# A macaron block (MoE FFN, attention, MoE FFN): a region per expert in the dispatch buffer, routing by batch, routed tiles in pairs, both FFNs' edges interleaved with attention

## The reference

```python
x = x + 0.5 * ffn(layernorm(x))        # routed and shared experts
x = x + attention(layernorm(x))        # 16 heads of 128, weights codes * scales
x = x + 0.5 * ffn(layernorm(x))

def ffn(flat):                          # 2048 tokens, 16 experts, top 2
    probs = softmax(flat @ router_w.T)
    topk_w, topk_idx = top_k(probs, 2);  topk_w = topk_w / sum(topk_w)
    shared = silu(flat @ shared_gate_w) * (flat @ shared_up_w) @ shared_down_w
    routed[t] = sum_k topk_w[t, k] * expert[topk_idx[t, k]](flat[t])
    return shared + routed              # an expert: silu(x @ gate) * (x @ up) @ down, inner width 128
```

## Time and profile before

| | us |
|---|---|
| median of 3 runs | 1320.77 (1317.02 to 1323.13) |
| span of the profiled execution | 1325.7 |
| PE busy in it | 1119.1 |
| DVE busy | 906.1 |
| ACT busy | 758.1 |
| POOL busy | 328.3 |

### The profile page before, as it was taken

How to read it: one execution, slowest core, us unless ns; L and a number is a source line. 1 busy time by engine, 2 the same in 40 slices (tenths; PEclk the granted TensorE clock), 3 DMA queues, 4 the chain that set the end, 5 groups by cost and what they waited for, 6 DMA issues and landing times. The chain is left out here.

```text
span 1325.7 us, 22540 instructions
## 1 busy us (share of the span) xinstructions
PE 1119.1 (84%) x5904; PEld 932.2 (70%) x5905; DVE 906.1 (68%) x1903; ACT 758.1 (57%) x1645; POOL 328.3 (25%) x421
## 2 busy tenths in 40 slices
PE   2556894589999999999999999999999994666884
PEld 1356783478888878888878887887888873455783
DVE  5654565677777777777777777777777778753554
ACT  3433551466767666666666676766676664433551
POOL 2174551750000351000144000042000001373551
PEclk9777997699999999999999999999999997877997
DMA  7563344430000131000032000028000001253435
GB/s 228 161 189 111 117 125 131 131 104 25 17 25 25 47 91 47 24 17 24 29 83 72 24 16 24 16 71 224 24 18 7 1 0 57 83 184 102 122 116 191
DMA packets 108557, 102.80 MB, mean 78 GB/s; under 512 B 13364, under 2 KB 97339, under 8 KB 108480
## 3 DMA queue, kind: packets, MB, share of 16 engines
q1 hardware_dynamic: 62880, 63.02, 17.1%
q10 hardware_dynamic: 37920, 22.07, 5.8%
q0 software_dynamic: 7680, 16.87, 3.4%
HBM read 54.55 MB, written 35.82 MB: 68 GB/s over the span
## 5 line engine op out<-in xcount | busy, mean ns | idle before, releaser
L198 PE MATMUL bank<-R 128*128 (+2 forms) x1056 | 416.6, 395 | 74.5 <-DVE R L539 47.2
L199 PE MATMUL bank<-R 128*128 (+2 forms) x1056 | 384.8, 364 | 0.0
L200 PE MATMUL bank<-R 128*128 (+2 forms) x1056 | 383.8, 363 | 0.0
L198 PEld LDWEIGHTS bank<-R 128*128 128x128 f32 x1056 | 207.8, 197 | 120.8 <-DVE R L539 43.7
L1048 DVE TENSOR_REDUCE a_mx<-bank 128x1 f32<-128x512 f32 x256 | 172.4, 691 | 99.5 <-PE bank L200 96.9
L200 PEld LDWEIGHTS bank<-R 128*128 128x128 f32 x1056 | 208.0, 197 | 29.7
L199 PEld LDWEIGHTS bank<-R 128*128 128x128 f32 x1056 | 208.9, 198 | 22.5
L974 ACT ACTIVATE work<-bank,a_mx 128x512 f32<-128x512 f32 x256 | 175.1, 688 | 55.3 <-DVE a_mx L1048 54.8
L980 ACT ACTIVATE R<-bank 128x512 fp32r<-128x512 f32 x256 | 139.1, 596 | 89.1 <-PE bank L1169 81.2
L1041 DVE SCALAR_TENSOR_TENSOR R<-bank,a_bslot,R 128x512 fp32r<-128x512 f32 x192 | 143.5, 747 | 64.6 <-ACT R L968 62.6
L1063 DVE TENSOR_TENSOR R<-bank,R 128x512 fp32r<-128x512 f32 x256 | 167.9, 680 | 11.0 <-ACT R L980 8.4
(11 more groups left out here) (137 smaller groups left out, 1528.1 us busy)
## 6 DMA issues: line engine op xcount, KB each, us to landing
R<-R ACTq DMA_DIRECT2D x60, 256.0 KB, 2.7
work<-in_ffn_w SPq DMA_DIRECT2D x54, 256.0 KB, 3.3
work<-xs_dram SPq DMA_DIRECT2D x96, 129.0 KB, 2.1
work<-y_dram SPq DMA_DIRECT2D x16, 512.0 KB, 5.0
work<-in_codes SPq DMA_DIRECT2D x64, 128.0 KB, 2.0
work<-in_scales SPq DMA_DIRECT2D x256, 32.0 KB, 1.8
xs_dram<-empty ACTq DMA_DIRECT2D x6, 1032.0 KB, 14.9
xs_dram<-empty SPq DMA_DIRECT2D x6, 1032.0 KB, 14.8
```

Of the source, the lines that this page charges most:

```text
L198: nc.tensor.matmul(out, ah, bh, start=(i == 0), stop=False)
L199: nc.tensor.matmul(out, ah, bl, start=False, stop=False)
L200: last = nc.tensor.matmul(out, al, bh, start=False, stop=(i == n - 1))
```

## The change

The kernel is written anew as one block with one instruction list per engine, and no hardware loops; every tile and unit is written out.

- **A region per expert.** `xs_dram` has 16 regions of 2048 + 128 rows, one for each expert, and 128 spare rows. A token's row is its region's base plus its rank in the expert, so that a batch's rows are known when the batches up to it are ranked. Rows are scattered per batch and choice (8 groups of 4). SP fills 128 rows behind each expert's last row with empty ones (16 DMAs at addresses read from `frow`), and loads tiles from addresses read from `toff`.
- **Routing by batch.** Statistics, normalizing, transposes, logits (now directly as [tokens, experts]), choice, ranks and positions run for one batch of four tiles after another. rstd comes by Ln and Exp on ACT and one Newton step.
- **Tiles in pairs.** 24 pairs instead of 48 tiles; one ACT or DVE operation for two tiles; a word is loaded for four tiles. ACT alone copies results out, without the weight; `combine` multiplies by the weight, 8 DVE operations a batch in place of 2. 16 tile buffers instead of 8.
- **Edges.** `EARLY` is 2. After the first FFN's tiles only batch 0 is combined, normalized and transposed before attention, and batch 1 while it starts; batches 2 and 3 follow at the end of units 0 and 2, and their transposes behind units 2 to 5. The attention's result is added to X directly (output projection as [tokens, values]: 12 matmuls of 256 columns for 6 of 512; no transposes back). The second FFN's statistics, transposes, logits, choices and positions of batches 0 to 2 run in units 52 to 63, its normalizing and scatters on POOL. All four shared steps come before the second FFN's tiles.
- **Weights of the second FFN.** The shared ones stay. The routed ones are split a second time by POOL during attention (16 experts, 768 columns), written to `w_dram`, and loaded as attention frees their place.

The core of the diff:

```diff
-NSLOT_TILES = (NTOK * TOPK + NE * (P - 1)) // P
-NR = -(-NSLOT_TILES // 4) * 4
+REGION = NTOK + P
+SPARE = NE * REGION
+XROWS = SPARE + P
+ROW = D + 1
+NR = 48
+NPAIR = NR // 2
...
+    x_load(0)
+    sp.dma_start(m.cst[:], t["consts"]).then_inc(s["cst_in"], 16)
+    x_load(1)
...
+    for c in range(2, NCHUNK):
+        chunk(c)
...
+    def fills(f):
+
+        sp.wait_ge(s[f"frow{f}"], 1)
+        for e0 in range(0, NE, 8):
+            _, at = nc.values_load_multi_w_load_instructions(
+                m.frow[0:1, e0:e0 + 8], engines=[SP_ENGINE], min_val=0, max_val=XROWS - P)
+            for v in at:
+                sp.dma_start(m.xs_dram[f][bass.ds(v, P), :], t["empty"]).then_inc(s[f"fill{f}"], 16)
...
+    fills(0)
+    tile_loads(0)
+    for n in range(4):
+        part(n)
+    results_landed(0)
+    y_loads(0, 0, 0)
...
+    weights(0)
+    for e in range(FIRST_PRE):
+        presplit(e)
+    weights(1)
...
+    for u in range(UNITS):
+        more = u + 1 < UNITS
...
+        act.wait_ge(s["o"], u + 1)
+        wait(act, s["y"], u)
...
+        if u in (0, 2):
+            b = 2 + u // 2
+            rstd("a", b)
+            normalize("a", b, xna(b), range(QB))
+        if u in (52, 56, 60):
+            rstd("1", (u - 52) // 4)
...
+        if u >= 4 and u % 4 == 0:
+            y_add(u // 4 - 1)
+        bias_lo(1, m.oT, "o", u, 2)
+        if u in (0, 2):
+            b = 2 + u // 2
+            combine(0, b, 0, 32 * (b + 1))
+            statistics("a", b)
+            rstd("a", b)
+        if u in (52, 56, 60):
+            q = (u - 52) // 4
+            dve.wait_ge(s["y_add"], 13 + q)
+            st.settle()
+            statistics("1", q)
+            rstd("1", q)
+        if u in L1_BEHIND and more:
+            choose(1, L1_BEHIND[u], te3(bank[0][:, 0:64]))
+        if u in R1_BEHIND:
+            positions(1, R1_BEHIND[u], te3(bank[0][:, 0:64]))
...
+    for step in range(2, QB):
+        gate_up(1, 2 * step)
+        gate_up(1, 2 * step + 1)
+        down(1, step)
+    pe.wait_ge(s["x_add"], 4 * QB)
+    pe.wait_ge(s["e_in"], 16 * NE)
+    tiles(1)
```

```diff
+    def behind_done(u):
+        if u in V_BEHIND:
+            pe.wait_ge(s["v_lo"], V_BEHIND[u] + 1)
...
+        if u in L1_BEHIND and u + 1 < UNITS:
+            pe.wait_ge(s["l_read1"], L1_BEHIND[u] + 1)
+        if u in R1_BEHIND:
+            pe.wait_ge(s["pos1"], TOPK * R1_BEHIND[u] + 1)
```

2224 lines of the change are left out of this document (1200 added, 1024 removed), and 4 rows, old and new, of the table SEMAPHORES.

## The result

The changed kernel takes 1341.41 us (median of 4 runs, 1340.65 to 1341.85); the kernel before took 1321.95 us beside it. The ratio is 1.0145, with an interval of 1.0123 to 1.0167: the change makes the kernel 1.5% slower. A second set of runs gave 1.0153 (1.0131 to 1.0174). The span of the profiled execution is 1338.8 us, 13.1 more than before.

The account below looks back on a forecast made before the run. TensorE was taken to bound attention and nearly the tile stages, chains the other stretches. Terms −15 + 1 − 17 + 58 − 36 + 1 + 2 = −6 gave a span of 1320, forecast 1315 us, range 1267 to 1349.

Parts of the forecast that it names:

- case A: The main forecast, the summed terms of all stretches: 1315 us, own range 1300 to 1330, chance 0.40.
- Attention, +58: Attention units: stalls from inserted DVE work, TensorE's additions and POOL's pre-split cost 58 us, bounds +30 and +80.
- the sign that I gave for a slower kernel: Attention: if unmarked units take over 13 us, the kernel is slower than forecast; they were expected at 12.8.
- The 5.5 us for 48 transposes: Attention: the added transposes counted among TensorE's own additions, 5.5 us.
- rival E: Attention and tile loops: straight code saves each loop turn its 2.07 us; −20, 1295 us, chance 0.05.
- First tile, 97: Before the first tile: SP's fills behind weight chunk 17 end the stretch at 97 us, −15; bounds 88 and 112.
- Tiles, +1 each: Both FFNs' tile stages: extra word loads cost 7 us, buffers and pairing save nearly that; +1 each, bounds −8 and +8.
- The two seams, −17 and −36: Last result to first unit shrinks to 49 us (−17); last unit to second FFN's first tile to 65 (−36).
- Tail, +2: Tail: DVE has 8 steps a batch instead of 2, but y loads and output set it; +2, bounds 0 and +5.
- B: Scatters set both tile starts, as DVE's waits overlap: first tile 91, last seam 50 us; 1289 us, chance 0.25.
- C: DVE's small steps stand behind POOL, 0.17 us more for each of some 144; +24, 1339 us, chance 0.22.
- D: Start: SP's fills and tile loads wait behind weight splits, so tiles start at 112 us; +13, 1328 us, chance 0.08.

Follow-up runs that it names:

- price: Changed kernel plus extra DVE steps in attention units where the change does nothing; read by unit: an insert of 2.71 us added 1.7, one of 16.46 added 17.7.
- price_warm: The kernel price plus unused TensorE matmuls in the stalls behind its inserts of 12 to 36 steps; the 36-step unit's extra time was 15.6 us, against 17.7.
- warm_real: Changed kernel plus unused TensorE matmuls in the long stalls of its own inserts (units 1, 3, 56, 57, 60, 61); ratio to before 1.0099, on another chip.
- t_price: Changed kernel plus four transposes in middle units, alone (0.5 us longer) or with ACT's copy and DVE's subtraction (1.9 to 2.0), and DVE steps with and without GpSimd.
- fills_early: Changed kernel with SyncE issuing the first FFN's first 8 fills after weight chunk 11, the others in pairs behind chunks 12 to 15; 1328.84 us, ratio to before 1.0039.
- words8: Changed kernel with TensorE loading expert words once for eight tiles instead of once for four; 1323.69 us, ratio to before 0.9996.
- all_edits: Changed kernel with its edge inserts cut into pieces and partly moved out, early fills and expert words for eight tiles; 1266.82 us, ratio to before 0.9582.
- fills_early_words8: Changed kernel with early fills and expert words loaded once for eight tiles, together, on the second chip; ratio to before 1.0028.

## Why the prediction was right or wrong

The forecast was 1315 and the result 1341.4, on the other side of before, though inside the range of 1267 to 1349. It lies outside case A's own range (1300 to 1330).

**Attention, +58 against +78: the step that failed.** The mechanism was right (a DVE insert is paid, and units 0, 2, 56 and 60 are at 22 us or more), but the sign that I gave for a slower kernel came true: ten unmarked units took 14 to 17 us and not 12.8. The slack was read too small: 0.39 of 1.36 us free by the earlier trace rows, where price has 1.05 free behind o_lo. The marked units hold 54 us where I had 41.6 of stalls, and part of that is the clock. Two terms were mis-sized for the worse. (1) The clock was not in the sum at all: each long stall costs 1.5 to 2.2 us on top (price, price_warm), by estimate 10 to 15 in all (warm_real). I had read the clock by stretches, in which the seams at 0.67 to 0.81 stood beside the attention's 1.00, and had not asked what puts it down. (2) The 5.5 us for 48 transposes were TensorE's own time; with ACT's copy and DVE's step in front of the last row maxima it is 1.6 to 1.8 a unit (t_price; 1.7 to 1.9 in units 1, 3, 53, 57 and 61) in ten units, some 12 us more. Two went the other way. (3) The output projection in 256 columns (+4.5) cost nothing; a middle unit still takes 12.73. (4) Straight code, which I counted as nothing, gave 4.6 (see rival E). GpSimd's pre-split was right with +1.4 against 1.5, and a logits matmul, for which I had no row and took 0.08 us, comes every 0.11. With these, 58 + 10 to 15 + 12 − 4.5 − 4.6 is 71 to 76, against 78 measured; the rest is not assigned.

**First tile, 97 against 107.8: failed.** DVE and GpSimd were as forecast: the last scatter was down at 90.2 (I had 89), the last weight chunk went out at 83. The mis-sized term is SyncE's: 16 fills at 0.90 us instead of 0.6, 14.4 us and not 10, issued from 86.1 on; then 5.0 us of landing and register loads, and another 2.2 until TensorE's first tile, where I had 4 together. fills_early, in which they stand elsewhere, has its first tile at 97.2.

**Tiles, +1 each against −1.9 and −5.8: failed, on the good side.** The gaps are there as forecast, ten a stage, 0.8 to 1.2 us. But the rest of a stage is faster: a pair without a load takes 2.8 to 3.0 us (rows of words8), 1.40 to 1.48 us a tile, below the 1.57 that I read from the rows of one tile. Over 48 tiles that is 4 to 8 us where I gave the pairs 3. The additional six word loads, for which I had 7 us, cost 8.2 a stage by words8 and hid most of it.

**The two seams, −17 and −36 against −19.7 and −34.8: right.** The DVE sum was right in its result. The last seam's working was not wholly right: DVE is busy for 38.3 of 66 us, and all_edits put 3.4 us more into it for 0.2. It is a chain of hand-overs between the shared steps with free time in it, not DVE's work.

**Tail, +2 against +2.3: right.**

**The rivals.** B (first tile 91, last seam 50) didn't come. C, the small steps beside GpSimd: added up over DVE's rows of up to 64 values, the time above the shortest of the same kind is 7 us ahead of the first tile and 3 behind it, not 24. Two of the steps, from DVE's timeline of the kernel after, beside GpSimd's subtractions:

```profile
27.28 1.47 DVE L843 TENSOR_TENSOR route<-route,cst 128x64 f32<-128x64 f32 x1
...
29.04 1.50 DVE L845 TENSOR_TENSOR route<-cst,rt 128x64 f32<-128x64 f32 x1
```

Later the 13 steps of a choice take 0.22 us each, as GpSimd stands idle or scatters while they run. By t_price the price per step beside GpSimd arithmetic would have been 0.44 us. So C ends near the time measured, but for another reason. D was near the truth for the first tile (112 against 107.8) and said why; its price is 112 − 97 = 15 and not the 13 that it was given. E, a gain by straight code, was real and small: the prediction said that the trace shows no loss at TensorE, and that was a wrong reading. Unit 23 of the kernel before has the loop's turn and no y_add behind it, and takes 13.67 us, where the two units ahead of it take 12.8 and 12.7:

```profile
583.95 0.69 ACT L1017 ACTIVATE R<-bank,a_bslot 128x512 fp32r<-128x512 f32 x1
...
587.34 0.69 DVE L1036 TENSOR_TENSOR R<-bank,R 128x512 fp32r<-128x512 f32 x1 [1.91 <-ACT R L961]
...
588.09 0.50 PE L198 MATMUL bank<-R 128*128 x1 [0.59 <-DVE R L1036]
...
597.62 0.69 ACT L1017 ACTIVATE R<-bank,a_bslot 128x512 fp32r<-128x512 f32 x1
```

ACT comes 2.07 us late, DVE's low part waits 1.91 us for it and TensorE 0.59 for that. The prediction compared it with a y_add unit of the same length, and that hid the loss. It happened at five turns, and the kernel after has none of it: 4.6 us in the attention. For the tile loops no run separates a turn from the load of a word. The slow case that came true was my forecast's own attention step at the upper end of its bounds (+80), which I had as a bound and not as a case.

**What the change is, then:** it moves three batches of work at each edge from seams, where TensorE waits anyway, into the stage where TensorE is the bound. It won 54 us there and paid 78. The work was not too much for the attention. In pieces of up to 1.4 us, and with half a batch's choice and a batch's positions left outside, it costs 26 to 34 us (units 844.8 and 853.3 against 818.9), and then the change is a gain.

## What to carry to other kernels

- Work that goes beside a bound engine has to be cut to the size of the waits that its host engine has in each period. Here 1.05 us in one place and 1.7 in another were free, and everything above was paid; the inserts of 4.08 us and longer cost 1.5 to 2.2 us more for TensorE's clock. Read the host's waits per unit before choosing a place, and count every queue: with the copy on ACT and the step on DVE a set of transposes cost more than three times TensorE's own 0.5 us.
- A move between two places is worth the difference of two prices, and both have to be measured where the work stands. Undoing each edge showed +36 against −29 and +51 against −52.
- Compare a unit only with a unit that does the same work. The unit with the loop's turn was as long as one with y_add, and so its 0.94 us looked like nothing.
- DMA issues and register loads at the end of a queue are serial time: 16 fills of 0.90 us cost 10 us because they stood behind the last weight chunk, and a word load costs 1.4 us on average, and 1.7 in the middle of a stage, where its gap shows 1.0.

## What the runs showed of the hardware

- The granted clock fell already in a unit with one insert of 4.08 us (0.90), and was 1.00 where TensorE had other matmuls in the stalls behind inserts of 7.5, 8.2 and 16.5 us, but 0.93 behind one of 10.97; the price of the fallen clock is 1.5 to 2.2 us a stall.
- A DVE step of 128x64 with two inputs from SBUF took 0.26 us with its hand-over alone and 0.70 beside GpSimd multiplications of 0.80 us each. The Trainium skill (SBUF — State Buffer, SBUF: two separate sides) says that the port pair is held by one of the two for a whole instruction, and that DVE steps with two SBUF inputs need it; the trace agrees, as each step took about as long as a GpSimd instruction.
- At five turns of the attention's loop ACT stood for 2.03 to 2.30 us (kernel before), and the unit there took 0.75 to 1.02 us longer than the same unit written out in the kernel after.
- Another chip behaved otherwise: the kernel before took 1353 us there instead of 1322. In all four kernels that ran there, DVE stood twice ahead of the first tile for 7 to 14 us, where on the first chip it doesn't (fills_early_words8, DVE's timeline):

```profile
66.71 0.22 DVE L876 TENSOR_TENSOR route<-bank,cst 128x64 f32<-128x64 f32 x1 [8.50 <-remote]
...
77.42 0.16 DVE L889 COPY tab<-bank 1x16 f32<-1x16 f32 x1 [7.96 <-issue]
```

  The profile names no engine and no transfer that ends these waits ("remote" for one, "issue" for the other), and the saving of words8 was gone there. No run separates the causes; it stays open.
